# The attention's first queries, keys and mask, worked out inside the last two batches of the key and value projections

## What is computed

```python
Q, K, V = proj(layernorm(x), W_q), proj(ctx, W_k), proj(ctx, W_v)      # 16 heads of 32
Q, K = rope(Q), rope(K)
scores = where(mask == 0, -inf, Q @ K.T / sqrt(32))
x = x + tanh(g_xattn) * (softmax(scores) @ V) @ W_o.T
aff = softmax(layernorm(x) @ gate_w.T)          # 8 experts, each takes its top 56 rows of a batch
x = x + tanh(g_ffn) * scatter_add(gating * expert(x_in))
```

## Time and profile before

| | |
|---|---|
| runs, median of 3 | 1874.7 us (1873.2 to 1875.49) |
| the profiled execution | 1875.96 us |
| its span | 1873.9 us |
| PE busy over the span | 1746.0 us (93%) |
| weight loads of PE | 1547.5 us (83%) |
| VectorE, ScalarE, GpSimd busy | 1044.8, 840.8, 203.4 us |
| mean granted clock of PE | 0.97 |

### The profile page before, as it was taken

How to read it: one execution, slowest core, us unless ns; L and a number is a source line. 1 busy time by engine, 2 the same in 40 slices (tenths; PEclk the granted TensorE clock), 3 DMA queues, 4 the chain that set the end, 5 groups by cost and what they waited for, 6 DMA issues and landing times.

```text
span 1873.9 us, 28462 instructions
## 1 busy us (share of the span) xinstructions
PE 1746.0 (93%) x10502; PEld 1547.5 (83%) x10502; DVE 1044.8 (56%) x1801; ACT 840.8 (45%) x1483; POOL 203.4 (11%) x286
## 2 busy tenths in 40 slices
PE   7999993899999999993799999999999999999995
PEld 6998982777778777762699999999999999999995
DVE  6566652778877877864353544535435354353541
ACT  3222221677767777770343433424434343343430
POOL 0000001212211211201100200102002020020101
PEclk9999996899999999996899999999999999999998
DMA  5545446567558567622433532525325352353421
GB/s 225 201 171 202 164 154 178 138 150 166 146 134 188 140 140 167 151 61 74 135 108 113 141 113 99 151 103 143 109 101 151 112 140 101 111 143 109 121 101 20
DMA packets 76187, 251.85 MB, mean 134 GB/s; under 512 B 10785, under 2 KB 10785, under 8 KB 74817
## 3 DMA queue, kind: packets, MB, share of 16 engines
q1 hardware_dynamic: 64096, 216.55, 38.0%
q0 software_dynamic: 12000, 34.12, 8.1%
HBM read 188.01 MB, written 51.61 MB: 128 GB/s over the span
## 4 chain that ended last, share of the span: by engine, by line
PE 51%; POOL 1%; DMA 0%; DVE 0%; issue 0%; DVEq 0%; ACT 0%; POOLq 0%
PE gu_ps L1381 11%; PE gu_ps L1379 11%; PE gu_ps L1380 11%; PE y_ps L1396 5%; PE y_ps L1397 5%; PE y_ps L1398 5%; PE y_ps L1407 1%; PE gu_ps L1365 1%; DMA xg<-xn_rows,gather_i 0%; POOL out L1239 0%; POOL xg L1229 0%; DVE xs_lo L1314 0%; DVE y_cols L1341 0%; PE gu_ps L1425 0%; DVE y_sb L1319 0%
## 5 line engine op out<-in xcount | busy, mean ns | idle before, releaser
L1379 PE MATMUL gu_ps<-xs_hi,ws_hi 128*128 128x448 f32 x1024 | 371.3, 363 | 3.0 <-DVE xs_lo L1314 3.0
L1381 PE MATMUL gu_ps<-xs_hi,ws_lo 128*128 128x448 f32 x1024 | 372.0, 363 | 0.0
L1380 PE MATMUL gu_ps<-xs_lo,ws_hi 128*128 128x448 f32 x1024 | 370.9, 362 | 0.0
L1309 DVE TENSOR_TENSOR ws_lo<-w_raw,ws_hi 128x1024 fp32r<-128x1024 f32 x192 | 235.2, 1225 | 189.8 <-ACT ws_hi L1259 189.2
L1259 ACT ACTIVATE ws_hi<-w_raw 128x1024 fp32r<-128x1024 f32 x192 | 201.7, 1050 | 165.1 <-PE y_ps L1398 146.6
L1050 PEld LDWEIGHTS t_ps<-cst,sm 112*125 112x125 f32 x1536 | 205.7, 191 | 73.7 <-issue 32.7
L1050 PE MATMUL t_ps<-cst,sm 112*125 112x112 f32 x1536 | 235.1, 282 | 19.4 <-DVE e_t L767 17.0
L759 DVE CUSTOM_DVE_ANT_0 sm<-m_ps,mq 112x752 f32<-112x752 f32 x256 | 229.9, 936 | 35.1 <-PE m_ps L1034 33.5
L653 ACT ACTIVATE sm<-sm,least 112x752 f32<-112x752 f32 x256 | 234.4, 917 | 19.0 <-DVE least L759 17.3
L1379 PEld LDWEIGHTS gu_ps<-xs_hi,ws_hi 128*128 128x128 f32 x1024 | 192.2, 188 | 15.5 <-issue 3.3
L1380 PEld LDWEIGHTS gu_ps<-xs_lo,ws_hi 128*128 128x128 f32 x1024 | 192.4, 188 | 14.2
(11 more groups left out here) (125 smaller groups left out, 2416.7 us busy)
## 6 DMA issues: line engine op xcount, KB each, us to landing
w_raw<-wstream SPq DMA_DIRECT2D x192, 512.0 KB, 3.5
ks<-k_split SPq DMA_DIRECT2D x192, 188.0 KB, 5.7
k_split<-k_split SPq DMA_DIRECT2D x32, 752.0 KB, 3.5
v_rows<-v_out SPq DMA_DIRECT2D x16, 750.0 KB
vs<-v_rows SPq DMA_DIRECT2D x16, 750.0 KB
c_raw<-ctxT SPq DMA_DIRECT2D x7, 1500.0 KB, 12.9
qs<-q_hi POOLq DMA_DIRECT2D x64, 112.0 KB, 5.4
mq_raw<-maskq SPq DMA_DIRECT2D x8, 656.2 KB, 10.7
```

Of the source, the lines that this page charges most:

```text
L1309: nc.vector.tensor_tensor(w_lo[s][:], w_raw[s][:], w_hi[s][:], ALU.subtract).then_inc(wlo_done[s], 1)
L1379: nc.tensor.matmul(o, w_hi[s][:, w], xs_hi[:, c], start=(c == 0), stop=False)
L1380: nc.tensor.matmul(o, w_hi[s][:, w], xs_lo[:, c], start=False, stop=False)
L1381: mm = nc.tensor.matmul(o, w_lo[s][:, w], xs_hi[:, c], start=False, stop=(c == DC - 1))
```

## The change

Batch 0's part of the functions `start` of the attention is moved into the projections. The two blocks share what it touches (the class `Both`), and since memory is full, several of these tiles lie where tiles of the projections lay: the first five `e_t` over the value and key output, `ks` over the raw context, `q_hi` and `q_lo` over nothing in use until the mask's own place `mq_first`, which lies over them.

- The values have three PSUM banks in place of four; the fourth, `q_ps`, takes the queries.
- `x` of batch 0 is loaded with the first inputs, its `moments` and `norm` stand between the first pair and the loop. W_q is loaded ahead of the loop.
- In batch 6, PE has `turn_x` behind values 0 and 1 and `project_q` behind values 2 and 3; ScalarE and VectorE have their parts beside it. VectorE does `moments` of batch 1 at its end.
- In batch 7, VectorE has `add_q`, `low_q`, and `norm` of batch 1; ScalarE has `high_q`; GpSimd stacks Q when `q_lo` is there, waits for all 12 transfers, and issues the mask's load; VectorE ends the block with `mask_queries`.
- SyncE issues the first two heads' keys ahead of batch 6 and six more heads' ahead of batch 7.
- SyncE does not wait for the stores at the end of the block. It waits for the value stores in the attention's block, ahead of `load_v`, and for the key stores behind the loads of W_o and the gate weights. ScalarE waits for all stores ahead of its first exponential, VectorE ahead of its first copy of a tile.

```diff
+KSLOTS = 2 * HG
+VBANKS = 3
+E_OVER = HG + 1
...
+        with ExitStack() as mid:
+            with ExitStack() as early:
+                wraw = sb(early, "wraw", [P, 2, DC, D])
+            with ExitStack() as early:
+                v_out = sb(early, "v_out", [KP, 2, KC, VH * DK])
+                k_split = [sb(early, f"k_split{j}", [P, 2, SK], F32R) for j in range(2)]
+            e_t = [sb(mid, f"e_t{j}", [KP, KC // 2, PAIR]) for j in range(E_OVER)]
+            with ExitStack() as early:
+                c_raw = [sb(early, f"c_raw{j}", [P, DC, S2]) for j in range(2)]
+            ks = sb(mid, "ks", [3 * WAYS, KSLOTS, SK], F32R)
+            with ExitStack() as early:
+                mq_first = sb(early, "mq_first", [QP, QC, S2], I32)
...
-        v_ps = [ps(st, f"v_ps{j}", [P, 512]) for j in range(4)]
+        v_ps = [ps(st, f"v_ps{j}", [P, 512]) for j in range(VBANKS)]
+        q_ps = ps(st, "q_ps", [P, 512])
...
                         if not last:
                             load_ctx(i + 1, j)
+                        elif j == 1:
+                            for h in (2, 4, 6):
+                                load_k(h)
...
+                def load_x(b):
+                    hold(xn_done, QC * b)
+                    sp.dma_start(x_t[:], x[b:b + 1].rearrange("o p c n -> p (o c) n")).then_inc(x_in, 16)
+
+                def load_k(h):
+
+                    for j in range(2 if h else 1):
+                        hold(ctx_lo[j], DC * B // 2)
+                    for r, part in ((0, 0), (1, 1), (2, 0)):
+                        sp.dma_start(both.ks[r * WAYS:r * WAYS + WAYS, h:h + 2].bitcast(F32),
+                                     kd[0:1, h % HG:h % HG + 2, part, h // HG * DK:h // HG * DK + DK].rearrange("o g d n -> d (o g) n")).then_inc(ks_in[h // 2], 16)
 
...
+                load_x(0)
                 pair(0, False)
+                sp.dma_start(wq_sb[:], wq).then_inc(wq_in, 16)
                 with sp.Fori(1, B // 2 - 1) as i:
                     pair(i, False)
-                sp.dma_start(wq_sb[:], wq).then_inc(wq_in, 16)
+                for s in range(2):
+                    hold(k_stored[s], 16 * NG // 2)
+                load_x(1)
+                load_k(0)
                 pair(B // 2 - 1, True)
-                for s in range(2):
-                    sp.wait_ge(k_stored[s], 16 * B * NG // 2)
-                for k in range(KC // VT):
-                    sp.wait_ge(v_stored[k], 16 * B)
...
+                nc.gpsimd.memset(minus_half[:], -0.5).then_inc(fill_set, 1)
+                nc.gpsimd.memset(mq[:, :, S2:SK], MASKED).then_inc(fill_set, 1)
...
+                hold(fill_set, 2)
+                root(0)
+                hold(consts_in, 32)
+                for n in range(2):
+                    hold(qrot_done, n + 1)
+                    half = q_rot[:, 2 * n:2 * n + 2]
+                    nc.gpsimd.tensor_tensor(half, half, q_sines[:, None, 0:S].broadcast_to((P, 2, S)), ALU.mult).then_inc(qsin_done, 1)
+                root(1)
+                hold(qlo_done, 1)
+                for g in range(NG):
+                    for r, part in ((0, q_hi), (1, q_hi), (2, q_lo)):
+                        pool.dma_start(qs[r * WAYS:r * WAYS + WAYS, g * HG:g * HG + HG, :].bitcast(F32),
+                                       part[g * DK:g * DK + DK].bitcast(F32)).then_inc(qs_in[g], 16)
+                for g in range(NG):
+                    hold(qs_in[g], 48)
+                pool.dma_start(both.mq_first[:], maskq[0:1].rearrange("o p c n -> p (o c) n")).then_inc(mq0_in, 16)
...
+                def x_columns(n):
+
+                    act.wait_ge(ahead_made, F_XT + n + 1)
+                    nc.scalar.activation(xT[:, n], q_ps[:, 0:2 * S], ACT.Copy).then_inc(ahead_free, 1)
+
+                def high_q():
+                    act.wait_ge(qsum_done, 1)
+                    nc.scalar.activation(q_hi[:], q_cos[:], ACT.Copy).then_inc(qhi_done, 1)
...
+                            if last and j == 0 and g in (0, 1):
+                                x_columns(g)
+                            if last and j == 1 and g == 1:
+                                high_q()
...
+                def mask_queries():
+                    dve.wait_ge(mq0_in, 16)
+                    dve.wait_ge(fill_set, 2)
+                    nc.vector.tensor_scalar(mq[:, :, 0:S2], both.mq_first[:], 0, MASKED, ALU.is_equal, ALU.mult).then_inc(mq_done, 1)
+
                 def pair(i, last):
                     for j in range(2):
                         for g in range(NG):
                             rotate(i, j, g, lambda: low_k(i, j, g - 1) if g else None)
                             if not (last and j):
                                 low_ctx(*following(i, j), g)
+                            if last and j == 0 and g == 2:
+                                turn_q(0)
+                            if last and j == 1:
+                                (add_q, low_q, lambda: norm(1), lambda: None)[g]()
                         low_k(i, j, NG - 1)
+                        if last and j == 0:
+                            turn_q(1)
+                            moments(1)
+                    if last:
+                        mask_queries()
...
+                moments(0)
+                norm(0)
...
-                    after(pe, v_copied, 2 * KC * i + KC * j + k - 3)
+                    after(pe, v_copied, 2 * KC * i + KC * j + k + 1 - VBANKS)
...
+                            if last and j == 0:
+                                if g < 2:
+                                    turn_x(g)
+                                else:
+                                    project_q(g - 2)
...
-                pair(0, True)
-                with pe.Fori(1, B // 2) as i:
-                    pair(i, False)
+                pair(0, True, False)
+                with pe.Fori(1, B // 2 - 1) as i:
+                    pair(i, False, False)
+                pair(B // 2 - 1, False, True)
...
                 def start():
-                    load_x(0)
-                    load_mq(0)
-                    load_k(0, 0)
-                    load_k(0, 2)
-                    load_k(0, 4)
+                    for k in range(KC // VT):
+                        hold(v_stored[k], 16 * B)
                     load_v(0, 0)
                     sp.dma_start(wo_sb[:], wo).then_inc(att_in, 16)
                     sp.dma_start(gw_sb[:], gatew).then_inc(att_in, 16)
-                    load_x(1)
+                    for k in range(2):
+                        hold(k_stored[k], 16 * B * NG // 2)
 
                 def body(b, j, first, last):
                     for t in range(0, H, 2):
                         if t + 6 < H:
-                            load_k(b, t + 6)
+                            if not first or t + 6 >= KSLOTS:
+                                load_k(b, t + 6)
...
-                    nc.gpsimd.memset(minus_half[:], -0.5).then_inc(fill_set, 1)
-                    nc.gpsimd.memset(mq[:, :, S2:SK], MASKED).then_inc(fill_set, 1)
-                    hold(fill_set, 2)
-                    root(0, 0, 0)
-                    for n in range(2):
-                        sines(0, n)
-                    for g in range(NG):
-                        stack_q(0, g)
-                    root(1, 0, 1)
+                    pass
...
-                    for n in range(2):
-                        x_columns(0, n)
-                    high_q(0)
+                    for k in range(KC // VT):
+                        act.wait_ge(v_stored[k], 16 * B)
+                    for k in range(2):
+                        act.wait_ge(k_stored[k], 16 * B * NG // 2)
...
                     nc.vector.memset(flags_sb[:], 0.0).then_inc(rest_free, 1)
-                    dve.wait_ge(x_in, 16)
-                    moments(0, 0, x_t)
-                    norm(0, 0, x_t, xn, xn_done)
-                    for n in range(2):
-                        turn_q(0, n)
-                    add_q(0)
-                    low_q(0)
-                    dve.wait_ge(fill_set, 2)
-                    mask_queries(0)
                     for h in range(MLEAD):
                         for qc in range(QC):
                             mask_scores(0, h, qc)
-                    next_moments(1)
-                    next_norm(1)
+                    for k in range(KC // VT):
+                        dve.wait_ge(v_stored[k], 16 * B)
+                    for k in range(2):
+                        dve.wait_ge(k_stored[k], 16 * B * NG // 2)
...
-                    for n in range(2):
-                        turn_x(0, n)
-                    pe.wait_ge(wq_in, 16)
-                    for n in range(2):
-                        for k in range(2):
-                            project_q(0, n, k)
```

More of the change, by code:

```diff
@@ L1 @@
 from contextlib import ExitStack
+from dataclasses import dataclass
 import concourse.bass as bass
@@ L62, in after @@
         eng.wait_ge(sem, value)
+F_XT, F_Q, F_USES = 0, 2, 4
+@dataclass
+class Both:
```

(43 more changed lines are left out.)

157 lines of the change are left out of this document (113 added, 44 removed).

## The result

| | before | after |
|---|---|---|
| runs of the comparison, median | 1873.95 us (4 runs, 1873.12 to 1875.49) | 1864.47 us (4 runs, 1861.66 to 1866.09) |
| the profiled execution, its span | 1875.96, 1873.9 us | 1861.66, 1859.8 us |
| PE busy, weight loads | 1746.0, 1547.5 us | 1738.0, 1542.7 us |
| VectorE, ScalarE, GpSimd busy | 1044.8, 840.8, 203.4 us | 1044.9, 840.6, 204.0 us |

What follows compares the result with a forecast made beforehand. One serial chain, 46.0 us from the last value copy to turn 0, was taken as the bound. Turn 0 sooner by 20.1 us, plus 2.7 and 1.0, made 23.8 us: forecast 1851.5 us, range 1846.5 to 1861.

Steps and rivals of the forecast that it cites:

- Projections: Batches 6 and 7: added PE work costs 7.2 us, last value copy at 288.3; VectorE's and ScalarE's added work costs nothing.
- The mask's chain: End of projections: stacking from 274.3, transfers landing 3.1 us after issue, mask at about 291, attention beginning at 292.5.
- the rival of that name: Before turn 0: the mask's chain governs if the mask lands after 300; with longest landings 1858.3 us; chance 0.12.
- the signs of being wrong: PE waiting in batches 6 and 7, the barrier coming after 300, or turn 0 beginning before 303.
- The store lands 7.6 us after its issue as before: Last value store, issued at 289.0, lands at 296.6, ahead of the value load.
- `att_in` 10.3 us later: Behind the store's landing, value load, W_o and gate weights take 10.3 us, complete at 306.9, releasing turn 0.
- Turn 0's worth: Start of attention: what turn 0 gains, the end gains; 307.0 in place of 327.15 gives 20.1 us.
- Ramp and clock: First turns: 2.7 us from moving batch 1's `moments` and `norm`, 1.0 us from the PE clock rising sooner.
- The five engines: Value store and load: a transfer of 125 partitions runs on about 5 of 16 DMA engines, 768 KB taking 6.0 us.
- The locking out of GpSimd: Stacking beside busy VectorE: two-port mode could delay it to the end of VectorE's projections; argued within the mask rival, 0.12.

Runs made afterwards that it cites:

- experiment 3: Changed kernel with the first mask's load issued ahead of the stacking transfers, without waiting for them; 1863.18 us, ratio 0.9949.
- experiment 4: As experiment 3, with the stacking of head groups 1 to 3 (9 of 12 transfers) issued once the value stores have landed; 1860.08 us.
- experiment 2: Changed kernel with SyncE waiting for W_o and gate weights to land before issuing the next x, keys and mask; 1860.31 us.
- experiment 1: Changed kernel with PE's wait for W_o and the gate weights moved from ahead of turn 0 to their first use in batch 1; 1850.35 us.
- run 6: Changed kernel with edits of experiment 1 and experiment 3, and transposed exponentials of heads 0 to 2 in tiles no store reads; 1850.58 us.
- run 8: As run 6, but W_o and gate weights issued ahead of the store's wait and PE's wait kept ahead of turn 0; 1849.38 us.
- run 9: As run 6, with x and keys of heads 8 and 9 ahead of the store's wait, mask at turn 6, weights at turn 8; 1844.11 us.
- runs 11 and 12: Run 9 with stacking of groups 2 and 3 behind the store's issue, 1844.06 us; then also SyncE waiting for the value load, 1844.46 us.

## Why the prediction was wrong

By its own steps:

- **Projections.** Right. Last copy forecast 288.3, found 288.00; store issued 289.0, found 288.67; PE busy 50 of 50 us. VectorE's query work cost nothing.
- **The mask's chain.** `low_q` and the start of stacking right (274.3, found 273.78); its transfers took up to 10.5 us to land, not 3.1, and the mask 10.1: block at 301, not 292.5. An error of 9 us that cost about 1, since the store covered it (experiment 3). The mask landed at 300.06, after the 300 from which on it was to govern by the rival of that name, and did not govern; the barrier at 301 is one of the signs of being wrong that the prediction had named.
- **"The store lands 7.6 us after its issue as before": the step that failed.** It measured 16.7 (14.4 to 16.6 in the runs with the same stacks). The prediction had the price of the store with nothing but stores and keys ahead, and put at nothing what the change itself moved in ahead of it: twelve stacking transfers, 1.38 MB, now fall at 273.8 to 280, with the issue of batch 7's *first* value store (277.17) in their midst and two key stores behind. Experiment 3 shows that both value stores were still to do at 290, experiment 4 that without nine of the stacks the time is 8.9 us.
- **"`att_in` 10.3 us later": mis-sized.** It measured 16.2. The three loads themselves take 12.5 (experiment 2), 2.2 more than forecast; the other 3.7 are x, keys and mask right behind them, which were left out although the order of the queue showed them. That no row showed the load alone was so for the rows, not for the trace: from 312 to 316 in the kernel before, just ahead of the gate weights' landing at 316.6, the share was 0.33 and 0.31 at 127 and 123 GB/s, as with the store.
- **Turn 0's worth.** Right, where it was tested. With turn 0 at 306.6 the time is 1850.35 (experiment 1). Sooner than that it is worth nothing by itself (run 6).
- **Ramp and clock.** 3.7 forecast, 15.5 - 11.5 = 4.0 found.

Together: 9.1 us from the store and 5.9 from the loads, less 0.3 from the issue, make 14.7, which is the 14.6 us by which turn 0 came later than 307.0. The time came only 13.0 us later than forecast: 0.3 of the difference is the ramp, 1.3 lie within the spread of the runs. The five engines hold up: the share is 0.31 to 0.33 whenever only value stores run. By the rule of the Trainium skill ("DMA: Bandwidth & Descriptors", section "Why a DMA increments its semaphore by 16 and not by 1"), 125 partitions go to five of the 16 engines, and a share of 5/16, 0.31, agrees with it. The load with nothing behind it, at most 9.1 us, is near the 7.6 of the store of its shape. The locking out of GpSimd that the same page of the Trainium skill names (section "SWDGE vs HWDGE vs iDMA") did not show: from 273.08 to 278.4 VectorE worked without a gap, and an issue in that stretch took 0.50 us (276.34), as before. Whether VectorE was in the mode that the page speaks of, no row tells.

What stays open: how the DMA engines share their time between GpSimd's transfers and SyncE's. Weights issued right behind the store left it its 15.0 us (run 8, for 15.3 in run 3), and x and keys there 15.8 (run 9), although the value load lost 6.5 us to what came behind it (runs 11 and 12). No run says why the one is delayed and the other not.

## What to carry to other kernels

When work is moved into a stage that looks idle on its engine, price its transfers against the transfers already in that stage, not only against the engine's queue: a store whose shape uses few DMA engines has a backlog long before the mean share shows it. A wait for several loads belongs at their first use, and bulk loads that nobody needs soon belong behind the small ones that somebody does; here, with the computation moved, one wait or one order was worth 14 us, more than the 9.5 of the move by itself. Each such repair uncovers the next late transfer, so follow the gain to the first later station at which it is gone.

## What was not expected

- Transfers issued *behind* a load on the same queue delayed it: the value load took at most 9.1 us with nothing behind it and 15.6 with 2.5 MB (two key loads of 564 KB, 750 KB of values and the mask of 656 KB) issued within 5 us behind it, one trace each; the gate weights, 16 KB, 11.7 us with nothing behind them and 15.4 with x, keys and mask. For the last value store the same did not show (runs 8 and 9).
- A store of 125 partitions moves 123 to 131 GB/s at a share of 0.31 to 0.33, and two of them in a row leave more than 11 us of work after everything else is done.
- 10 us that turn 0 gained were worth nothing (run 6 against run 1: 1850.58 and 1850.35), although at turn 2 they were still there (the first quad's reciprocal at 307.73 for 317.72): a transfer at turn 5, and the lower clock behind it, took them.
